# TensorE's order in an attention loop: both halves of the value products between two pairs of score tiles

## The chip, the cores and the metric

The kernel runs on 1 core of one Trainium2 chip. The metric is device time in microseconds of one execution, lower is better; the figure given is the median of several executions.

## What is computed

A pre-norm attention block followed by a pre-norm FFN with values rounded to fp8, on x of shape (4, 1024, 128), 16 heads of size 8:

```
proj = layernorm(x) @ w_in;  k, v, q = split(proj)
scores = q k^T / sqrt(8) + tisa_bias(head, j - i)      # the bias depends on j - i alone
attn   = softmax(scores) v
x = x + a * sigmoid(g),  (a, g) = split(attn @ w_gate + b_gate)
x = x + ffn(layernorm(x))                              # 128x128, both operands rounded to fp8
```

The change lies in the loop that makes scores, their softmax numerators and the products with v.

## The kernel before

A **group** is 128 keys of one head, for all 4 batches and all 1024 queries of each. A head has 8 groups (`GPH`), 16 heads make 128 groups. The loop `Fori(0, NH2)` on every engine takes two heads (16 groups) a turn, 8 turns. Numbers within a group are the batches b = 0 to 3.

Work of a group, and who does it:

- TensorE, `scores(i, g, b)`, L909 to L940: for one batch two matmuls (L928), one for each half of the queries, into two PSUM banks. For b = 0, 1, 2 ("by vector", `DPG` = 3) the tile goes alternately to banks 0-1 and 2-3 (`unit(k)`, k counts such tiles). Before tile k TensorE waits (L920) until VectorE has read tile k-2, for the same banks. For b = 3 the tile goes to banks 4-5, after a wait (L924) for ScalarE's exponential of b = 3 of the group before; four more matmuls (L937) then add the bias as identity times the table `t64`. I call these "the identity bias".
- VectorE, `add_bias`, L987: for b = 0, 1, 2 reads the score tile from PSUM, adds the bias table and writes to a buffer in SBUF (`pbuf` or `split`, 4 groups deep, `SETS`).
- ScalarE: exponential in place for b = 0, 1, 2 (L1030), and from PSUM for b = 3 (L1038), strictly in the order 0, 1, 2, 3.
- TensorE, `products(i, g, c)`, L942 to L959: for one half c of the queries, 4 matmuls of fp32 data (each one recorded as two), one for each batch, v (with a column of ones for the denominators) against the exponentials, accumulated over the head's 8 groups in bank 6+c. c = 0 waits (L946) for the exponentials of the whole group; for the first group of a head each half also waits (L951) until the sums of the last head have been copied out of the bank.

TensorE runs scores two groups ahead of products (`LAG` = 2): at step g it issues the scores of group g+2 and the products of group g. Within a step its order is written out by hand at L967: score tile 0, products half 0, score tile 1, products half 1, score tiles 2 and 3 with the identity bias. Each engine's queue runs in order; nothing behind a waiting instruction of TensorE starts before it.

Once per head VectorE copies bank 6 (L779, after half 0 of the head's last products, `half_done`) and ScalarE copies bank 7 (L780, after half 1). SyncE and GpSimd load the next head's tables and normalise the last head's sums; none of that is touched.

Of the kernel before, what the change touches and what calls it, by code (L numbers as in the profile page):

```python
# [62 lines left out]
def attention_block(nc, io, out):  # L63
    with ExitStack() as ctx:
# [238 lines left out]
        with nc.Block() as block:  # L303
# [91 lines left out]
            def _(eng):  # L395
# [41 lines left out]
                def bias_copies(_):  # L437
                    eng.wait_ge(gsum_ready, 1)
                    eng.activation(gvh[:, :], ps[:, 0, :], ACT.Copy).then_inc(gh_ready, 1)
                    eng.activation(gv[:, :], ps[:, 0, :], ACT.Copy).then_inc(gh_ready, 1)  # L440
# [5 lines left out]
                def high_keys(_):  # L446
                    eng.wait_ge(kh_ready, B)
                    load_keys(eng, 2, (0, 8), 1)
# [344 lines left out]
        def slot(g, b):  # L793

            n = 4 * (g % SETS) + b
            return pbuf[:, n, :] if n < 8 else splitf[:, (n - 8) * S:(n - 7) * S]

        def unit(k):

            return 2 * (k % 2)  # L800
# [16 lines left out]
        with nc.Block() as block:  # L817
# [89 lines left out]
            @block.tensor  # L907
            def _(eng):
                def scores(i, g, b):  # L909

                    p, t = (g // GPH) % 2, g % GPH
                    by_vector = b < DPG
                    if b == 0 and t == 0:
                        eng.wait_ge(head_in[p], (i + (g // (2 * GPH))) * (16 * LOADS) + 16 * LOADS)
                    if by_vector:
                        k = DPG * g + b
                        u = unit(k)

                        if k >= 2:
                            eng.wait_ge(z_ready, i * (2 * DPH) + (k - 1))  # L920
                    else:
                        u = 4
                        if g:
                            eng.wait_ge(p_ready, i * (8 * GPH) + 4 * g)  # L924
                    keys = slice(b * S + t * P, b * S + (t + 1) * P)
                    for c in range(2):
                        rows = slice(ROW * c, ROW * c + 33)
                        last = eng.matmul(ps[:, u + c, :], kb[p][rows, keys],  # L928
                                          qb[p][rows, b * HALF:(b + 1) * HALF],
                                          start=True, stop=True)  # L930
                    if by_vector:
                        last.then_inc(sd_ready, 1)
                        return
                    for c in range(2):
                        for m in range(2):
                            c0 = t * P + 64 * m + c * HALF
                            last = eng.matmul(ps[64 * m:64 * m + 64, u + c, :], ident2[:, :],  # L937
                                              t64[p][:, c0:c0 + HALF], start=False, stop=True,
                                              skip_group_check=True)
                    last.then_inc(sp_ready, 1)  # L940

                def products(i, g, c):  # L942

                    p, t = (g // GPH) % 2, g % GPH
                    if c == 0:
                        eng.wait_ge(p_ready, i * (8 * GPH) + 4 * (g + 1))  # L946
                        if t == 0:
                            eng.wait_ge(vst_in, i * 2 + (p + 1))
                    if t == 0:

                        eng.wait_ge(o_ready[c], i * 2 + (p + 1))  # L951
                    for b in range(B):
                        last = eng.matmul(ps[32 * b:32 * b + 32, 6 + c, :], vst[p][:, b * TB + t, :],  # L953
                                          slot(g, b)[:, c * HALF:(c + 1) * HALF],
                                          start=(t == 0), stop=(t == TB - 1))
                    if c == 1:
                        last.then_inc(groups_done, 1)
                    elif t == TB - 1:
                        last.then_inc(half_done, 1)  # L959

                for g in range(LAG):
                    for b in range(B):
                        scores(0, g, b)
                with eng.Fori(0, NH2) as i:
                    for g in range(2 * GPH):

                        for steps, c in (((0,), 0), ((1,), 1), ((2, 3), None)):  # L967
                            if g < 2 * GPH - LAG:
                                for b in steps:
                                    scores(i, g + LAG, b)  # L970
                            else:

                                with eng.If(i < NH2 - 1):
                                    for b in steps:
                                        scores(i, g + LAG, b)
                            if c is not None:
                                products(i, g, c)

            @block.vector
# [578 lines left out]
```

## Time and profile before

| what | us |
|---|---|
| median of 3 executions | 625.23 |
| lowest, highest | 624.38, 629.33 |
| the profiled execution | 625.92 |
| its span in the trace | 624.1 |

The rows of the profile are given further down. They name engines as PE (TensorE's matmuls), PEld (its weight loads), DVE (VectorE), ACT (ScalarE), POOL (GpSimd) and SP (SyncE). A matmul row merges the matmuls of one kind that follow each other: x8 of L953 is one half of the products of one group, x2 of L928 is one score tile. The loop's score groups start at 68.5 us of the span, and its last products end at 562 us.

### The profile page before, as it was taken

The page shows a single profiled execution, that of the slowest core. Times are in us where ns is not written, and L with a number is a line of the kernel's source. Part 1 is how long each engine was busy: PE and PEld are TensorE (multiplying, and loading weights), DVE is VectorE, ACT ScalarE, POOL GpSimd, SP SyncE. Part 2 cuts the span into 40 slices and gives each one's busy share as a digit, 9 for nine tenths or more (in the row PEclk, how much of TensorE's full clock was granted, in tenths as well). Part 3 has the DMA queues.
Part 4 walks back from the last instruction along what each step waited for, and adds up shares of the span by engine and source line. Part 5 has one row for each costly group of instructions (what it writes and reads, how often), then busy time and mean ns, then how long its engine had stood idle before and what let it go on. Part 6 is the DMA issues. An engine that isn't in the chain of part 4 may idle for free.

```text
span 624.1 us, 12700 instructions
## 1 busy us (share of the span) xinstructions
PE 576.9 (92%) x4003; PEld 157.9 (25%) x4003; DVE 552.1 (88%) x691; ACT 553.4 (89%) x615; POOL 88.3 (14%) x90
## 2 busy tenths in 40 slices
PE   4887499999999999999999999999999999999945
PEld 1534012222222222222222222222222222224532
DVE  6763599999999999999999999999999999974885
ACT  5663499999999999999999999999999999983475
POOL 4170400010101010101010101001010101011640
PEclk8797599999999999999999999999999999999958
DMA  7117620514141424232332323231414141410004
GB/s 178 67 22 206 223 65 2 149 20 148 32 133 42 123 59 109 79 90 87 81 102 63 104 61 110 55 117 49 121 45 123 43 133 39 124 23 9 1 0 135
DMA packets 29484, 52.63 MB, mean 84 GB/s; under 512 B 9438, under 2 KB 20699, under 8 KB 28507
## 3 DMA queue, kind: packets, MB, share of 16 engines
q1 hardware_dynamic: 27496, 51.70, 29.2%
q10 hardware_dynamic: 1970, 0.73, 0.6%
q8 instruction: 8, 0.13, 0.1%
q14 instruction: 10, 0.07, 0.0%
HBM read 42.35 MB, written 9.16 MB: 83 GB/s over the span
## 4 chain that ended last, share of the span: by engine, by line
ACT 43%; issue 36%; PE 9%; DVE 4%; SPq 3%; DMA 2%; ACTq 1%; DVEq 0%
ACT split L1030 17%; ACT pbuf L1030 17%; ACT pbuf L1038 3%; PE ps L1232 3%; ACT split L1038 2%; PE ps L585 1%; SPq L301 1%; DMA amp<-in_L_attn_amplitudes 1%; DMA kb<-split 1%; SPq L262 1%; PE ps L953 1%; PE ps L1227 1%; ACT o_sbs L780 1%; PE ps L928 1%; PE ps L575 1%
## 5 line engine op out<-in xcount | busy, mean ns | idle before, releaser
L987 DVE TENSOR_TENSOR split<-ps,t 128x1024 f32<-128x1024 f32 x192 | 231.4, 1222 | 13.0 <-PE ps L928 7.6
L987 DVE TENSOR_TENSOR pbuf<-ps,t 128x1024 f32<-128x1024 f32 x192 | 230.2, 1217 | 11.8 <-PE ps L928 6.9
L1030 ACT ACTIVATE pbuf<-pbuf 128x1024 f32<-128x1024 f32 x192 | 206.7, 1255 | 8.6 <-DVE pbuf L987 8.3
L1030 ACT ACTIVATE split<-split 128x1024 f32<-128x1024 f32 x192 | 202.2, 1263 | 1.2 <-DVE split L987 1.2
L928 PE MATMUL ps<-qb,kb 33*128 33x512 f16 x1024 | 184.1, 390 | 13.3 <-SPq L845 6.4
L953 PE MATMUL ps<-pbuf,vst 128*32 128x512 f32 x1024 | 137.2, 608 | 0.0
L953 PE MATMUL ps<-split,vst 128*32 128x512 f32 x1024 | 136.0, 604 | 1.0 <-ACT split L1038 1.0
L928 PEld LDWEIGHTS ps<-qb,kb 33*128 33x128 f16 x1024 | 48.6, 93 | 300.7 <-DVE pbuf L987 114.1
L937 PE MATMUL ps<-t64s,ident 128*64 128x512 f16 x512 | 80.5, 395 | 0.0
L1038 ACT ACTIVATE split<-ps 128x1024 f32<-128x1024 f32 x64 | 78.3, 1223 | 0.0
L1038 ACT ACTIVATE pbuf<-ps 128x1024 f32<-128x1024 f32 x64 | 77.9, 1218 | 0.0
L905 POOL TENSOR_TENSOR o_sbs<-o_sbs,rd 128x1024 f32<-128x1024 f32 x8 | 19.1, 2390 | 179.6 <-DMA rd<-r_scratch 179.6
L899 POOL TENSOR_TENSOR o_sbs<-o_sbs,rd 128x1024 f32<-128x1024 f32 x7 | 16.7, 2388 | 157.9 <-DMA rd<-r_scratch 157.9
L953 PEld LDWEIGHTS ps<-split,vst 128*32 128x32 f32 x1024 | 20.3, 108 | 31.5 <-issue 29.7
L953 PEld LDWEIGHTS ps<-pbuf,vst 128*32 128x32 f32 x1024 | 20.2, 108 | 29.2 <-issue 29.2
L937 PEld LDWEIGHTS ps<-t64s,ident 128*64 128x64 f16 x512 | 18.1, 108 | 31.2 <-issue 31.2
L277 POOL COPY vst<-v_all 128x256 f32 (+1 forms) x16 | 6.4, 398 | 120.0 <-PE ps L953 98.3
L1314 ACT ACTIVATE pbuf<-ps 128x256 f32<-128x256 f32 x16 | 6.0, 381 | 14.8 <-PE ps L1232 14.8
L1232 PE MATMUL ps<-wgate,v_all 128*128 128x256 f32 x64 | 18.1, 405 | 0.0
L1164 POOL TENSOR_TENSOR x_sb<-x_sb,pbuf 128x256 f32<-128x256 f32 x16 | 11.5, 724 | 29.1 <-DVE pbuf L1431 29.1
L1431 DVE TENSOR_TENSOR pbuf<-ps,pbuf 128x256 f32<-128x256 f32 x16 | 6.6, 415 | 8.9 <-ACT pbuf L1314 8.9
L780 ACT ACTIVATE o_sbs<-ps 128x512 f32<-128x512 f32 x16 | 12.7, 792 | 2.0 <-PE ps L953 2.0
(151 smaller groups left out, 325.4 us busy)
## 6 DMA issues: line engine op xcount, KB each, us to landing
t<-g_scratch SPq DMA_DIRECT2D x16, 960.0 KB
kb<-k_scratch SPq DMA_DIRECT2D x120, 64.0 KB
t64s<-gh_scratch SPq DMA_DIRECT2D x16, 248.0 KB
t64s<-gl_scratch SPq DMA_DIRECT2D x16, 248.0 KB
qb<-q_scratch SPq DMA_DIRECT2D x60, 64.0 KB
x_sb<-in_L_attn_x SPq DMA_DIRECT2D x4, 512.0 KB, 7.6
q_scratch<-split SPq DMA_DIRECT2D x8, 256.0 KB, 3.9
k_scratch<-split SPq DMA_DIRECT2D x8, 256.0 KB, 3.8
```

Of the source, the lines that this page charges most:

```text
L780: return eng.activation(dst, src, ACT.Copy)
L899: eng.tensor_tensor(o_sb[1], o_sb[1], rd[:, :], ALU.mult).then_inc(o_norm, 1)
L905: eng.tensor_tensor(o_sb[0], o_sb[0], rd[:, :], ALU.mult).then_inc(o_norm, 1)
L928: last = eng.matmul(ps[:, u + c, :], kb[p][rows, keys], qb[p][rows, b * HALF:(b + 1) * HALF], start=True, stop=True)
L937: last = eng.matmul(ps[64 * m:64 * m + 64, u + c, :], ident2[:, :], t64[p][:, c0:c0 + HALF], start=False, stop=True, skip_group_check=True)
L953: last = eng.matmul(ps[32 * b:32 * b + 32, 6 + c, :], vst[p][:, b * TB + t, :], slot(g, b)[:, c * HALF:(c + 1) * HALF], start=(t == 0), st ...
L987: eng.tensor_tensor(slot(g, b), banks(unit(k), 2), t128[p][:, t * P:t * P + S], ALU.add).then_inc(z_ready, 1)
L1030: eng.activation(buf, buf, ACT.Exp).then_inc(p_ready, 1)
L1038: eng.activation(buf, banks(4, 2), ACT.Exp).then_inc(p_ready, 1)
L1164: eng.tensor_tensor(xs, xs, gate[:, j % NG, :], ALU.add).then_inc(x1_ready, 1)
L1232: last = eng.matmul(ps[:, j % 4, m * 2 * D:(m + 1) * 2 * D], num[n // TB][:, (n % TB) * P:(n % TB + 1) * P], wgate[:, :], start=False, sto ...
L1431: eng.tensor_tensor(gate[:, j % NG, :].rearrange("p (m d) -> p m d", d=D), ps[:, j % 4, :].rearrange("p (m c) -> p m c", c=2 * D)[:, :, 0: ...
```

## The change

Within a step TensorE issues score tiles 0 and 1 together, then both halves of the products, then score tiles 2 and 3 and the identity bias. The waits stay with the functions that issue them, the number of instructions of each kind is the same, and no other engine's program changes.

```
-                        for steps, c in (((0,), 0), ((1,), 1), ((2, 3), None)):
+                        for steps, halves in (((0, 1), (0, 1)), ((2, 3), ())):
                             if g < 2 * GPH - LAG:
                                 for b in steps:
                                     scores(i, g + LAG, b)
@@
                                 with eng.If(i < NH2 - 1):
                                     for b in steps:
                                         scores(i, g + LAG, b)
-                            if c is not None:
+                            for c in halves:
                                 products(i, g, c)
```

## Rows read from the trace of the kernel before

**Rows 1.** The page's first part: busy time of each engine, its share of the span

```profile
PE 576.9 (92%) x4003; PEld 157.9 (25%) x4003; DVE 552.1 (88%) x691; ACT 553.4 (89%) x615; POOL 88.3 (14%) x90
```

**Rows 2.** The page's groups: busy, mean ns of one, idle before and its releaser

```profile
L987 DVE TENSOR_TENSOR pbuf<-ps,t 128x1024 f32<-128x1024 f32 x192 | 230.2, 1217 | 11.8 <-PE ps L928 6.9
```

**Rows 3.** Windows: length, busy of PE, PEld, DVE, ACT, POOL, clock, DMA share, GB/s

```profile
68.50:76.50 8.00, 5.97 (x24) 1.06 (x24) 6.71 (x6) 5.80 (x6) 4.32 (x6) 0.50 0.64 237
150.00:300.00 150.00, 148.31 (x1104) 32.94 (x1102) 144.76 (x129) 150.00 (x164) 13.94 (x10) 1.00 0.30 84
```

**Rows 4.** Timeline of PE over one step: start us, length us, then the instructions

```profile
304.77 0.63 PE L928 MATMUL ps<-qb,kb 33*128 33x512 f16 x4
305.33 0.62 PE L937 MATMUL ps<-t64s,ident 128*64 128x512 f16 x4
305.89 0.39 PE L928 MATMUL ps<-qb,kb 33*128 33x512 f16 x2
306.21 1.06 PE L953 MATMUL ps<-pbuf,vst 128*32 128x512 f32 x8
307.20 0.39 PE L928 MATMUL ps<-qb,kb 33*128 33x512 f16 x2
307.52 1.06 PE L953 MATMUL ps<-pbuf,vst 128*32 128x512 f32 x8
308.52 0.39 PE L928 MATMUL ps<-qb,kb 33*128 33x512 f16 x2
```

**Rows 5.** Timeline, narrow windows in the same step: single instructions of PE, ACT, DVE

```profile
305.01 0.39 PE L928 MATMUL ps<-qb,kb 33*128 33x512 f16 x2
303.68 1.28 ACT L1038 ACTIVATE pbuf<-ps 128x1024 f32<-128x1024 f32 x1
305.21 1.23 DVE L987 TENSOR_TENSOR pbuf<-ps,t 128x1024 f32<-128x1024 f32 x1
306.41 1.22 DVE L987 TENSOR_TENSOR split<-ps,t 128x1024 f32<-128x1024 f32 x1
```

**Rows 6.** Timeline, early in the loop: PE's tile 0, and ACT's L1038

```profile
81.42 0.39 PE L928 MATMUL ps<-qb,kb 33*128 33x512 f16 x2
103.78 0.39 PE L928 MATMUL ps<-qb,kb 33*128 33x512 f16 x2
82.98 1.01 ACT L1038 ACTIVATE split<-ps 128x1024 f32<-128x1024 f32 x1
105.45 1.03 ACT L1038 ACTIVATE pbuf<-ps 128x1024 f32<-128x1024 f32 x1
```

**Rows 7.** Timeline at the loop's end: both halves of the last products, and DVE's copy

```profile
560.17 1.92 PE L953 MATMUL ps<-split,vst 128*32 128x512 f32 x16 [0.95 <-ACT split L1038]
561.30 0.69 DVE L779 COPY o_sbs<-ps 128x512 f32<-128x512 f32 x1 [3.47 <-PE ps L953]
```

**Rows 8.** Timeline: a score tile of PE that waited for DVE

```profile
106.43 1.22 DVE L987 TENSOR_TENSOR pbuf<-ps,t 128x1024 f32<-128x1024 f32 x1
107.70 0.39 PE L928 MATMUL ps<-qb,kb 33*128 33x512 f16 x2
```

**Rows 9.** Timeline around the two copies at a head's end, DVE and ACT

```profile
440.75 0.68 DVE L779 COPY o_sbs<-ps 128x512 f32<-128x512 f32 x1
441.35 2.34 DVE L987 TENSOR_TENSOR pbuf<-ps,t 128x1024 f32<-128x1024 f32 x2
441.53 1.32 ACT L1030 ACTIVATE pbuf<-pbuf 128x1024 f32<-128x1024 f32 x1
442.96 1.33 ACT L1030 ACTIVATE pbuf<-pbuf 128x1024 f32<-128x1024 f32 x1
```

**Rows 10.** Timeline at the low clock: a score tile, half 0, the next score tile

```profile
76.53 0.61 PE L928 MATMUL ps<-qb,kb 33*128 33x512 f16 x2
77.06 1.93 PE L953 MATMUL ps<-pbuf,vst 128*32 128x512 f32 x8
78.93 0.47 PE L928 MATMUL ps<-qb,kb 33*128 33x512 f16 x2
```

More of the change, by code:

```diff
@@ L965, in _ @@
                     for g in range(2 * GPH):
-                        for steps, c in (((0,), 0), ((1,), 1), ((2, 3), None)):
+                        for steps, halves in (((0, 1), (0, 1)), ((2, 3), ())):
                             if g < 2 * GPH - LAG:
@@ L975, in _ @@
                                         scores(i, g + LAG, b)
-                            if c is not None:
+                            for c in halves:
                                 products(i, g, c)
```

## The prediction

> **What bounds the kernel now.** I read the page first, then windows by stage, then the timeline of single steps. The page shows three engines that are nearly even: PE 92%, DVE 88%, ACT 89% of the span [rows 1], and DVE's adds have little idle before them, 11.8 us for 192 of them [rows 2]. An average can't tell which of them is the bound, so I looked at the windows: in 150 us of the loop PE is busy for 148.31, ACT for all 150.00, DVE for 144.76, at clock 1.00 [rows 3]. The loop is the place to look; the change touches nothing outside it.
>
> The timeline of one step gives its shape. Call score tiles S0 to S3, the identity bias I, the halves P0 and P1. From S2 at 304.77 to the next S2 at 308.52 are 3.75 us, and PE goes through it without a hole: S2 to S3 0.24 (305.01), S3 to I 0.32, I to S0 0.56, S0 to P0 0.32, P0 to S1 0.99, S1 to P1 0.32, P1 to S2 1.00 [rows 4, 5]. Is PE the bound? Early in the loop it ran by itself: S0 at 81.42 and at 103.78 are 6 groups apart, 3.73 us a group. Over the same groups ACT's L1038 ended at 83.99 and at 106.48: 22.49 us for 6, 3.75 a group [rows 6]. So ACT is the slower one; it fell behind until S3, which needs the banks that ACT reads in L1038, had to wait for it: ACT ends at 303.68 + 1.28 = 304.96, S3 starts at 305.01 [rows 5]. From then on all go at ACT's 3.75, with PE only 0.02 faster on its own. DVE has the most room: back to back its adds start 1.13 apart (two in 2.34, the second taking 1.21 [rows 9]), and 1.20 where it goes from S2 to S0 (305.21 to 306.41 [rows 5]), 3.46 a group.
>
> Per head the copies add to this. ACT starts its next exponential at 442.96, 1.43 after the one at 441.53, where a quarter of a group is 0.94: 0.49 later [rows 9]. A head takes about 8 x 3.75 + 0.49 = 30.5 us.
>
> **What the change does to PE's own time.** Nothing is added or removed, no DMA or other queue is passed. Four neighbour pairs change. Before: S0-P0, P0-S1, S1-P1, P1-S2. After: S0-S1, S1-P0, P0-P1, P1-S2. S0 to S1 now costs what S2 to S3 does, 0.24. P0 with P1 directly behind exists at the loop's end: 16 records in 1.92 against 1.06 for one half [rows 7, 4], so the second half adds 0.86; and since a half of 1.06 is followed by the next score tile 1.00 after its start, both take 1.86 from P0's start to S2. PE's own step becomes 0.24 + 0.32 + 1.86 + 0.24 + 0.32 + 0.56 = 3.54, against 3.75: 0.21 saved.
>
> The Trainium skill ("TensorEngine Tiling (Array Packing)", Key Properties) says that a change of tiling mode drains TensorE, and scores and products here differ in mode; the rows fit, with 0.99 from half to score tile where half to half is 0.86. By that rule with PE as the bound the loop's 125 steps would give back 26 us. The rule is not wrong, but the time saved is not on the path, for two reasons.
>
> First, ACT needs 3.75 a group whatever PE does. So a quicker PE alone gives nothing.
>
> Second, and this decides, the new order puts a wait at a bad place. S1 is tile k+2 to S2 of the group before (the order on DVE's banks is S0, S1, S2, S0', S1'), so S1' needs the banks of S2, which DVE must have read (L920). Count from S2's start:
>
> - S2 to DVE's start on it: 304.77 to 305.21, 0.44 as read; 0.43 is what single records and the step's sums agree on [rows 4, 5]
> - DVE's add: 1.23 [rows 5]
> - DVE's end to the score tile that waits for it: 106.43 + 1.22 = 107.65 to 107.70, 0.05 [rows 8]
>
> So S1' cannot start before S2 + 1.71. Before the change it started at S2 + 2.43 (307.20), since P0 stood ahead of it: 0.72 of slack, the wait was free. After, PE is ready for it at 0.24 + 0.32 + 0.56 + 0.24 = 1.36 and stands still for about 0.35 to 0.4. Behind it in the queue stand P0 and P1, whose data is long there, and behind them S2', which is what DVE needs next. So a closed chain forms:
>
> S2 -0.43-> DVE -1.23-> -0.05-> S1' -0.32-> P0, P1 -1.86-> S2': 3.89 us a group.
>
> DVE has S0' and S1' to do meanwhile: S0' starts at 0.43 + 1.20 = 1.63, S1' at 2.76, and DVE could take S2' at 3.89, but gets it at 3.89 + 0.43 = 4.32. It idles 0.4 a group, PE about 0.35 to 0.4, ACT 0.14. Before, the longer way round (S2' 3.75 after S2) never closed, as two small waits lay apart.
>
> Could another wait bite as well? S2' needs DVE to be done with S0': 1.63 + 1.22 = 2.85, it starts at 3.89. S3' needs ACT's L1038. ACT can take S2's tile at 1.7, then L1038 0.94 later, done by 2.64 + 1.28 = 3.92 at the longest length seen; S3' is due at 3.89 + 0.24 = 4.13. P0 needs exponentials of two groups earlier, more than 3 us old. None bites.
>
> **Sum.** The loop issues scores for groups 2 to 127, so 125 intervals from S2 to S2. 118 go from 3.75 to 3.89: +16.5. The first seven went at 3.73: 7 x 0.16 = +1.1. The head's end happens 15 times in the loop: DVE's copy of bank 6 waits for P0, which ends later now. P0 starts at S2 + 1.71 + 0.32 = 2.03; at the loop's end the copy started 1.13 after P0 did [rows 7], so at 3.16. After the copy DVE's add follows 0.60 later (440.75 to 441.35), the one for S2' 1.13 behind it [rows 9]: 4.89 instead of 4.32. That is +0.57 a head, and ACT's copy (0.49) fits under it. The old cost of 0.49 goes, so 15 x 0.08 = +1.2. The first step of the loop, at the low clock, has two switches fewer: about -0.2. Together **+18.6 us**. The profiled execution took 625.92, so 644.5; it lies 0.7 above the median of 625.23, which goes to **644 us**.
>
> Bounds. If going from half 0 to half 1 within the loop costs as a change of weights between two passes does, 0.45 twice instead of 0.43 (1.06 less the last record's 0.61), 0.05 more a group: +6, 650. The two handoffs (0.43 and 0.05) are each seen with an error of 0.02: 125 x 0.04 = 5 either way. If the copy waits for nothing new, 1.2 less. Both low ends together give 638, both high ends 655; as the rows of the loop's end show the two halves directly, I cut the top to 652.
>
> **Rivals.**
>
> - *The wait costs nothing, the time stays (625).* It needs the closed chain under 3.75, that is 0.14 shorter than its rows. For: PE gains 0.21 a step. Against: each term was read where it stands alone, and the chain holds no part of what PE gains except P0-P1. Then ACT at 3.75 decides and no time is won. Chance 7%.
> - *PE was the bound, the switches' time is won.* Place: the changes between score and product; price 0.21 x 125 = 26, so 599 (the page on tiling would have it so); it decides only if ACT can go under 3.75, and DVE's chain too. In no group did ACT do so [rows 6]. Chance 2%.
> - *The clock falls.* PE stands still 0.35 to 0.4 us each 3.89. At clock 0.50, while PE was busy 5.97 of 8.00 us [rows 3], a half took 1.87 to the next score tile (77.06 to 78.93), tile to half 0.53, and a tile's record 0.61 for 0.39 [rows 10, 4], so S2 to DVE 0.43 + 0.22: a step would take about 0.53 + 2 x 1.87 + 0.65 + 1.23 + 0.05 = 6.2 us. One group in ten at that clock adds 12.5 x 2.3 = 29 us: 673. Against: PE will still be busy some 93% of each step, in even pieces. Chance 4%. The Trainium skill ("TensorE: Matmul & The Clock Gate", A second HAM failure mode: psum-queue depth-cycling) tells of a kernel whose small idles between groups of matmuls for want of PSUM banks made the clock swing; that is this rival's case, and the trace of before has no such swing in the loop.
> - *The chain holds but with another length, outside 638 to 652.* For instance, DVE's late copy delays two steps of a head, not one (another 15 x 0.4 = 6), or PE's loads restart slower after a real stall. Chance 12%.
>
> My forecast, the closed chain at 3.84 to 3.94: 75%. What this kernel's measurement can tell from no change is about 1%. Slower by over 1%: 75 + 4 + 12 = 91, less 1 for a chain much shorter than thought, 90%. Same 8%, faster 2%.
>
> **What the profile of after would show.** Steps 3.89 apart from S2 to S2. PE idle of about 0.35 to 0.4 ahead of S1 in every step, released by DVE L987, with S1 0.05 behind DVE's end on S2's tile. PE's busy in 150:300 down from 148 to about 140. Idle of DVE before its adds to `pbuf` up from 11.8 us [rows 2] to 25 to 32, released by PE L928. ACT no longer busy all the time, its L1038 records back from 1.28 [rows 5] to the 1.01 to 1.03 of the first groups [rows 6], since nothing queues in it. S0 to S1 0.24, P0 and P1 as one row of 16 with 1.92. Wrong would be: S1 ahead of DVE's end by more than the wait allows, steps of 3.75 with ACT still full, or a granted clock under 1.00 inside the loop.

## The result, and the profile after

The changed kernel took 646.69 us (median of 4, 645.96 to 649.2) against 625.87 for the kernel before in the same session (median of 4): a ratio of 1.033, with an interval of 1.030 to 1.036. So it is 3.3% slower. The forecast was 644 us, 638 to 652. One execution of the kernel before, in the session of e1, e3, e4 and e5, took 2132.34 us and is left out of the ratios.

The profiled execution has a span of 644.5 us, 20.4 more than before. The page's first part, and the groups that answer to [rows 1] and [rows 2]:

```profile
PE 563.8 (87%) x4003; PEld 160.3 (25%) x4003; DVE 544.9 (85%) x691; ACT 569.1 (88%) x615; POOL 88.3 (14%) x90
...
L987 DVE TENSOR_TENSOR pbuf<-ps,t 128x1024 f32<-128x1024 f32 x192 | 226.8, 1216 | 22.2 <-PE ps L928 21.5
L928 PE MATMUL ps<-qb,kb 33*128 33x512 f16 x1024 | 178.9, 388 | 46.9 <-DVE pbuf L987 24.1
```

TensorE lost 13 us of busy time and yet the span grew. VectorE waits 22.2 us for score tiles (L928) before its adds to `pbuf`, where it waited 11.8 us before [rows 2], and TensorE's score tiles wait for VectorE: each waits for the other, which is what a closed chain looks like in the groups. The window answers to [rows 3]; its columns are the same:

```profile
150.00:300.00 150.00, 138.68 (x1062) 32.55 (x1054) 136.81 (x123) 148.71 (x157) 13.91 (x10) 1.00 0.26 74
```

PE fell from 148.31 to 138.68, DVE from 144.76 to 136.81, ACT from 150.00 to 148.71, at clock 1.00 as before. No engine is full any more; ScalarE's 148.71 still looks full, but the length of its records is not its pace (last section). One step on the timelines of PE and DVE, against [rows 4, 5]:

```profile
441.57 0.61 PE L928 MATMUL ps<-qb,kb 33*128 33x512 f16 x4
442.10 0.62 PE L937 MATMUL ps<-t64s,ident 128*64 128x512 f16 x4
442.66 0.39 PE L928 MATMUL ps<-qb,kb 33*128 33x512 f16 x2
443.28 0.39 PE L928 MATMUL ps<-qb,kb 33*128 33x512 f16 x2 [0.23 <-DVE pbuf L987]
443.60 1.92 PE L953 MATMUL ps<-pbuf,vst 128*32 128x512 f32 x16
445.46 0.39 PE L928 MATMUL ps<-qb,kb 33*128 33x512 f16 x2
442.00 1.23 DVE L987 TENSOR_TENSOR pbuf<-ps,t 128x1024 f32<-128x1024 f32 x1 [0.36 <-PE ps L928]
443.18 2.36 DVE L987 TENSOR_TENSOR split<-ps,t 128x1024 f32<-128x1024 f32 x2
445.89 1.23 DVE L987 TENSOR_TENSOR split<-ps,t 128x1024 f32<-128x1024 f32 x1 [0.35 <-PE ps L928]
```

S2 starts at 441.57. VectorE takes it at 442.00 (0.43 later) and is done at 443.23 (1.23). S1 starts at 443.28 (0.05), the halves at 443.60 (0.32), the next S2 at 445.46 (1.86). The sum is the step: 3.89. The chain that ended last, cut to 430 to 450 us, by line:

```profile
by line: PE ps L953 46.3%; DVE split L987 24.7%; PE ps L928 20.0%; DVE pbuf L987 12.4%; issue 1.8%
```

It runs through the products, the adds and the score tiles, the terms of the sum; ScalarE has no part in it.

### The profile page after: what moved, and what is told of

The parts are those of the page before. It is cut to its first block, busy times and chain, and to the rows that moved or that the text cites. A ratio compares the mean times of both kernels' runs of the same rounds, so it can differ in the third digit from the quotient of the medians.

```text
span 644.5 us, 12684 instructions
## 1 busy us (share of the span) xinstructions
PE 563.8 (87%) x4003; PEld 160.3 (25%) x4003; DVE 544.9 (85%) x691; ACT 569.1 (88%) x615; POOL 88.3 (14%) x90
## 4 chain that ended last, share of the span: by engine, by line
PE 58%; DVE 29%; issue 5%; SPq 3%; DMA 2%; ACT 2%; DVEq 0%; ACTq 0%
PE ps L953 35%; PE ps L928 14%; DVE pbuf L987 13%; DVE split L987 12%; PE ps L1232 2%; PE ps L1276 1%; PE ps L585 1%; SPq L301 1%; DMA amp<-in_L_attn_amplitudes 1%; DMA kb<-split 1%; SPq L262 1%; PE ps L1227 1%; PE ps L575 1%; DVE amax L1462 1%; DMA v_all<-last_rows 1%
## 5 line engine op out<-in xcount | busy, mean ns | idle before, releaser
L987 DVE TENSOR_TENSOR pbuf<-ps,t 128x1024 f32<-128x1024 f32 x192 | 226.8, 1216 | 22.2 <-PE ps L928 21.5
L928 PE MATMUL ps<-qb,kb 33*128 33x512 f16 x1024 | 178.9, 388 | 46.9 <-DVE pbuf L987 24.1
L1030 ACT ACTIVATE pbuf<-pbuf 128x1024 f32<-128x1024 f32 x192 | 197.2, 1052 | 11.1 <-DVE pbuf L987 8.2
L1030 ACT ACTIVATE split<-split 128x1024 f32<-128x1024 f32 x192 | 195.4, 1052 | 3.8 <-DVE split L987 2.1
L953 PE MATMUL ps<-pbuf,vst 128*32 128x512 f32 x1024 | 124.8, 606 | 0.0
L953 PE MATMUL ps<-split,vst 128*32 128x512 f32 x1024 | 123.1, 598 | 0.7 <-ACT split L1038 0.7
L928 PEld LDWEIGHTS ps<-qb,kb 33*128 33x128 f16 x1024 | 39.2, 93 | 246.7 <-issue 139.9
L1038 ACT ACTIVATE pbuf<-ps 128x1024 f32<-128x1024 f32 x64 | 64.5, 1007 | 0.0
L1038 ACT ACTIVATE split<-ps 128x1024 f32<-128x1024 f32 x64 | 64.5, 1007 | 0.0
L953 PEld LDWEIGHTS ps<-pbuf,vst 128*32 128x32 f32 x1024 | 26.9, 110 | 53.8 <-issue 53.8
L953 PEld LDWEIGHTS ps<-split,vst 128*32 128x32 f32 x1024 | 26.7, 109 | 54.4 <-issue 52.3
L779 DVE COPY o_sbs<-ps 128x512 f32<-128x512 f32 x16 | 11.1, 692 | 8.4 <-PE ps L953 8.4
```

What stands on the lines that cost most here:

```text
L779: return eng.tensor_copy(dst, src)
L928: last = eng.matmul(ps[:, u + c, :], kb[p][rows, keys], qb[p][rows, b * HALF:(b + 1) * HALF], start=True, stop=True)
L987: eng.tensor_tensor(slot(g, b), banks(unit(k), 2), t128[p][:, t * P:t * P + S], ALU.add).then_inc(z_ready, 1)
L1030: eng.activation(buf, buf, ACT.Exp).then_inc(p_ready, 1)
L1038: eng.activation(buf, banks(4, 2), ACT.Exp).then_inc(p_ready, 1)
```

## The experiments

All times below are medians, and the kernel before is 625.22 to 627.53 in the runs beside them. "Head's end" is the step in which the last sums of a head are copied out.

### Is it the wait behind VectorE's add? (e3)

```
# from the changed kernel; VectorE, then ScalarE
+                    w = HALF if b == 2 else S
-                    eng.tensor_tensor(slot(g, b), banks(unit(k), 2), t128[p][:, t * P:t * P + S],
+                    eng.tensor_tensor(slot(g, b)[:, 0:w], banks(unit(k), 2)[:, 0:w], t128[p][:, t * P:t * P + w],
...
-                                eng.activation(buf, buf, ACT.Exp).then_inc(p_ready, 1)
+                                eng.activation(buf, buf, ACT.Exp, scale=0.0 if b == 2 else 1.0).then_inc(p_ready, 1)
```

> The changed kernel, but VectorE adds the bias for the first 512 of 1024 columns of tile 2 only, and ScalarE's exponential of tile 2 (still 1024 columns) has scale 0, so its values are all 1: part of the computation is left out. Theory (closed chain): VectorE's add of tile 2 falls from 1.23 to about 0.69 and the chain from 3.89 to 3.35, below ScalarE's 3.75, which then sets the step as before the change, with 0.49 more at each head's end: 625, 622 to 629. TensorE waits for ScalarE ahead of S3, not for VectorE ahead of S1. Rival (the halves together are slow in themselves, or ScalarE is slowed by the new order): 647, as ScalarE and TensorE have the same work.

Measured: 626.75 us, a ratio to the kernel before of 1.000 (0.998 to 1.002). All of the loss is gone, though TensorE and ScalarE have the same instructions to do. The timeline of PE; the fifth line is a narrow window that shows S3 alone:

```profile
431.41 0.61 PE L928 MATMUL ps<-qb,kb 33*128 33x512 f16 x4
431.94 1.92 PE L953 MATMUL ps<-pbuf,vst 128*32 128x512 f32 x16
433.80 0.87 PE L928 MATMUL ps<-qb,kb 33*128 33x512 f16 x4
434.60 0.62 PE L937 MATMUL ps<-t64s,ident 128*64 128x512 f16 x4
434.28 0.39 PE L928 MATMUL ps<-qb,kb 33*128 33x512 f16 x2
435.16 0.39 PE L928 MATMUL ps<-qb,kb 33*128 33x512 f16 x2
```

S0 and S1 follow each other without a hole; the only wait is S3's for its banks (S3 starts 0.48 behind S2, 433.80 to 434.28, where 0.23 would do without a wait), and the step is 3.75 (431.41 to 435.16). With the chain shortened, ScalarE sets the step again, as in the kernel before. This shows that the chain through VectorE's add costs the time, not the halves standing together in themselves. It also shows that the new order gains nothing while ScalarE needs 3.75.

### Does the new order save TensorE anything? (e4, e5)

```
# e4 from the changed kernel, e5 from the kernel before: the cuts of e3, and
+                                w = HALF if b == 1 else S
+                                eng.activation(buf[:, 0:w], buf[:, 0:w], ACT.Exp,
+                                               scale=0.0 if b == 2 else 1.0).then_inc(p_ready, 1)
```

> As the last kernel, and ScalarE's exponential of tile 1 is done for 512 of 1024 columns only: part of the computation is left out. With the chain at 3.35 and ScalarE at about 3.3 a step, TensorE's own time sets the step. Theory (the new order does save TensorE 0.21 to 0.23 a step): 0.23 + 0.32 + 1.86 + 0.23 + 0.31 + 0.24 + 0.31 = 3.50 a step, 125 x 0.25 = 31 us under 625, and some of the 15 x 0.49 of ScalarE's copy covered: 588, 584 to 598. Rival (changing between scores and products costs nothing that the order can save): as e5, near 616.

> The kernel before the change, with the same two cuts (VectorE's add of tile 2 and ScalarE's exponential of tile 1 for 512 columns only, the exponential of tile 2 with scale 0): part of the computation is left out. TensorE's own time with the old order sets the step: 3.73, as in groups 3 to 9 of the kernel before. 118 x 0.02 = 3 less, and ScalarE's copy of 0.49 at 15 head ends is covered: 7 less: 616, 612 to 620. e4 should lie 22 to 30 us below it, 125 steps of 0.21 to 0.23. Rival: both the same.

Measured: e4 593.35, e5 615.37 us; ratios to the kernel before 0.946 (0.943 to 0.949) and 0.983 (0.978 to 0.987). With VectorE's and ScalarE's limits lifted, the new order is the quicker by 22 us. PE's timeline of e4, then of e5:

```profile
401.63 0.61 PE L928 MATMUL ps<-qb,kb 33*128 33x512 f16 x4
402.17 1.92 PE L953 MATMUL ps<-split,vst 128*32 128x512 f32 x16
404.02 0.61 PE L928 MATMUL ps<-qb,kb 33*128 33x512 f16 x4
...
405.12 0.39 PE L928 MATMUL ps<-qb,kb 33*128 33x512 f16 x2
```

```profile
415.93 0.39 PE L928 MATMUL ps<-qb,kb 33*128 33x512 f16 x2
416.25 1.07 PE L953 MATMUL ps<-split,vst 128*32 128x512 f32 x8
417.25 0.39 PE L928 MATMUL ps<-qb,kb 33*128 33x512 f16 x2
417.57 1.06 PE L953 MATMUL ps<-split,vst 128*32 128x512 f32 x8
...
419.65 0.39 PE L928 MATMUL ps<-qb,kb 33*128 33x512 f16 x2
```

A step is 3.49 (401.63 to 405.12) against 3.72 (415.93 to 419.65). TensorE's saving is real, 0.23 to 0.24 a step: 125 x 0.24 = 30 us. Of this 8 us go back at the heads' ends: in e4 the step from 415.57 takes 3.64 and the one from 419.20 takes 3.86 against 3.48 of the others, so 0.54 a head and 15 x 0.54 = 8; in e5 the same steps take 3.73 like all. This cost at the heads' ends is why e4 came out at 593 and not at 588.

### Is it where the two halves stand, or S0 with S1? (e1)

```
-                        for steps, halves in (((0, 1), (0, 1)), ((2, 3), ())):
+                        for steps, halves in (((0,), (0, 1)), ((1, 2, 3), ())):
```

> Order in a step: S0, P0, P1, S1, S2, S3, I; no other change. The pair that the change put together, S0 with S1, is apart again; both halves still stand together. Theory (closed chain through VectorE's two pairs of banks): the tile ahead of the halves is now S0 and the tile behind them S1, and S0' needs the banks of S1. S1 to VectorE 0.43, add 1.23, 0.05 to S0', 0.32 to P0, 1.86 to S1': 3.89 us a step again, with TensorE's wait ahead of S0 in place of S1. Here S1, S2 and S3 follow each other, so ScalarE's exponential of tile 3 ends late: S1 + 0.43 + 1.23 + 0.03 (exponential of tile 1), 1.13 later tile 2, 0.95 later tile 3, 1.01 long, 0.06 to the next S3: that S3 starts at 4.84 in place of 4.34, and a step takes (4.84 + 0.86 + 2.18) / 2 = 3.94. The copy at a head's end is hidden more than in the changed kernel (about 0.3 for 0.67). Sum: 125 x 0.05 - 15 x 0.37 = +1 on the 646.7 of the changed kernel: 648, 642 to 653. Rival (the loss comes from S0 and S1 standing together ahead of the products): back to about 625.

Measured: 648.45 us, a ratio of 1.034 (1.031 to 1.037), the same loss as the changed kernel's, and 648 was worked out. PE's timeline over two steps:

```profile
444.06 0.39 PE L928 MATMUL ps<-qb,kb 33*128 33x512 f16 x2
444.38 1.92 PE L953 MATMUL ps<-pbuf,vst 128*32 128x512 f32 x16
446.23 0.61 PE L928 MATMUL ps<-qb,kb 33*128 33x512 f16 x4
447.19 0.39 PE L928 MATMUL ps<-qb,kb 33*128 33x512 f16 x2 [0.35 <-ACT pbuf L1038]
...
448.06 0.39 PE L928 MATMUL ps<-qb,kb 33*128 33x512 f16 x2
...
450.24 0.61 PE L928 MATMUL ps<-qb,kb 33*128 33x512 f16 x4
451.08 0.39 PE L928 MATMUL ps<-qb,kb 33*128 33x512 f16 x2 [0.23 <-ACT split L1038]
...
451.95 0.39 PE L928 MATMUL ps<-qb,kb 33*128 33x512 f16 x2
```

S0 starts at 444.06, 448.06 and 451.95: steps of 4.00 and 3.89 in turn, mean 3.95, where 3.94 was worked out. S3 waits for ScalarE in both, for longer in the 4.00 (0.35 in the records against 0.23). So the mean step here is set by the longer way round that was worked out before the run: from S1 over VectorE's add and three exponentials to S3 of the next step, and from there over both halves to S1 of the step after. The chain through VectorE alone lies just under it: in the shorter steps S0 comes 1.71 behind S1 (450.24 to 451.95), which is its 0.43 + 1.23 + 0.05. That S0 and S1 are apart again brings nothing back. What the two orders share is that both halves stand between two neighbouring VectorE tiles.

### Does work count more inside the chain? (e2)

```
-                        for steps, halves in (((0, 1), (0, 1)), ((2, 3), ())):
+                        for steps, halves in (((0, 1), (0, 1)), ((3, 2), ())):
```

> The changed kernel with tiles 2 and 3 exchanged: S0, S1, P0, P1, S3, I, S2. TensorE has the same instructions and nearly the same own time, about 3.5 a step. Theory (closed chain): S3 and I now lie between the halves and S2, inside the chain: S3 to I 0.31, second pair of I 0.24, to S2 0.32, so 0.86 more a step: 4.75. At the head's end VectorE's copy is hidden by VectorE's longer idle, 15 x 0.67 less. 646.7 + 108 - 10 = 745, 735 to 755. Rival (the time is TensorE's work plus a fixed cost of the halves standing together): no change, 647.

Measured: two runs only, 774.31 us with a mean granted clock of 0.93 and 797.40 us with 0.90, beside 625.22 us for the kernel before with 0.95 to 0.96. Both are more than the 735 to 755 expected; the profile is of the longer one. PE's timeline, first of a step at the full clock, then of one that ran partly at the low clock; then two windows (columns as in [rows 3]):

```profile
600.06 0.60 PE L928 MATMUL ps<-qb,kb 33*128 33x512 f16 x4
601.77 0.39 PE L928 MATMUL ps<-qb,kb 33*128 33x512 f16 x2 [1.11 <-DVE split L987]
602.09 1.92 PE L953 MATMUL ps<-pbuf,vst 128*32 128x512 f32 x16
603.95 0.39 PE L928 MATMUL ps<-qb,kb 33*128 33x512 f16 x2
604.27 0.62 PE L937 MATMUL ps<-t64s,ident 128*64 128x512 f16 x4
604.82 0.60 PE L928 MATMUL ps<-qb,kb 33*128 33x512 f16 x4
...
429.64 0.60 PE L928 MATMUL ps<-qb,kb 33*128 33x512 f16 x4
431.35 0.39 PE L928 MATMUL ps<-qb,kb 33*128 33x512 f16 x2 [1.11 <-DVE pbuf L987]
431.67 3.39 PE L953 MATMUL ps<-pbuf,vst 128*32 128x512 f32 x16
436.05 0.61 PE L928 MATMUL ps<-qb,kb 33*128 33x512 f16 x4
...
432.00:435.30 3.30, 3.30 (x18) 0.54 (x10) 1.56 (x2) 3.19 (x4) 1.12 (x1) 0.50 0.16 22
150.00:600.00 450.00, 354.88 (x2432) 79.86 (x2432) 312.99 (x283) 341.56 (x359) 29.82 (x22) 0.92 0.22 63
```

At clock 1.00 the step is 4.76 (600.06 to 604.82); 4.75 was worked out: the same instructions, 0.87 a step longer, since the identity bias now lies between the halves and S2. TensorE stands idle 1.11 us a step. And here what was a rival of the prediction happened: the clock fell. In the step from 429.64 to 436.05 the clock was 0.50 from 432.0 to 435.3, the lower of its two levels (1.2 and 2.4 GHz); the halves took 3.39 for 1.92, and the step 6.41. Over 150 to 600 us the mean clock was 0.92 with PE busy 79% of the time. After the loop's first step, 29 steps are of that kind, 6.3 to 6.5 us each; together they cost 48 us of the profiled run's 797, and without them it would be about 750, inside the range expected. From 575 to 664 us the steps were of the same 4.76 us and the clock stayed at 1.00; what decides when it falls, these runs do not show.

### The head's end (e6)

```
# VectorE, for both heads of a turn; from the changed kernel
-                            if b == 0 and g == LAG - 1:
+                            if b == 1 and g == LAG - 1:
...
-                            if b == 0 and g == GPH + LAG - 1:
+                            if b == 1 and g == GPH + LAG - 1:
```

> The changed kernel, with VectorE's copy of bank 6 at a head's end put after its add of tile 1 in place of tile 0; the computation is the same. By the trace of the changed kernel each head's end costs 0.67 over a plain step, since VectorE stands idle until half 0 is done before it can copy. Theory: after tile 1 half 0 is long done, the copy (0.61) falls into VectorE's idle time of 0.42 ahead of tile 2, and 0.19 is left: 15 x 0.48 = 7 less: 639.5, 637 to 643. Rival (the 0.67 comes from ScalarE's copy of bank 7): 646 to 648.

Measured: 639.98 us, a ratio of 1.022 (1.019 to 1.024), so 6.7 us less than the changed kernel (7 us by the two ratios, 1.033 and 1.022, each taken against the kernel before in its own session). First VectorE around the copy in the changed kernel, then in e6:

```profile
456.49 0.69 DVE L779 COPY o_sbs<-ps 128x512 f32<-128x512 f32 x1 [0.42 <-PE ps L953]
457.10 2.35 DVE L987 TENSOR_TENSOR pbuf<-ps,t 128x1024 f32<-128x1024 f32 x2
```

```profile
452.50 0.68 DVE L779 COPY o_sbs<-ps 128x512 f32<-128x512 f32 x1
453.09 1.21 DVE L987 TENSOR_TENSOR pbuf<-ps,t 128x1024 f32<-128x1024 f32 x1
```

In the changed kernel VectorE stood 0.42 in front of the copy, waiting for half 0 (L953), with the adds behind it. In e6 the copy starts without a wait. The heads' ends cost 0.67 each before and 0.15 to 0.25 now, by the distances between S0s over two steps. ScalarE's copy was not touched, so it was not the cause.

## Why the prediction was right

**The bound of the kernel before.** Argued from ScalarE's pace in the first groups; shown by e3 (ScalarE alone holds the step at 3.75 when the chain is short) and by e5 (with less work for ScalarE and VectorE the old order runs at 3.72 to 3.73, TensorE's own time, which was forecast as 3.73).

**TensorE's own saving.** Forecast 0.21 a step; e4 against e5 shows 0.23 to 0.24. The small miss is that S0 to S1 and S2 to S3 take 0.23 and S3 to the identity bias 0.31 where nothing waits; the row of before, with 0.24 and 0.32, had S3 waiting. The Trainium skill ("TensorEngine Tiling (Array Packing)", Key Properties) says that a change of tiling mode drains TensorE. The runs agree so far as fewer changes between scores and products are worth 0.23 to 0.24 a step; whether a drain is what costs it, they do not show. In the changed kernel the time was lost all the same, which was the point of the two reasons given.

**The closed chain.** Term by term: S2 to VectorE 0.43 (forecast 0.43), add 1.23 (1.23), to S1 0.05 (0.05), to the halves 0.32 (0.32), both halves 1.86 (1.86); the step 3.89 (3.89). This carried 17.6 of the 18.6 us forecast. e3 and e2 test it from two sides: a term shortened, and the chain lengthened by 0.86. e1 moves it by one tile and rules out that S0 with S1 costs the time, but its mean step is set by the longer way round through ScalarE, so it is no test of the 3.89.

**The head's end.** This term was sized too small. Forecast was 0.57 a head, 0.67 is measured. TensorE's timeline has the parts:

```profile
455.27 1.92 PE L953 MATMUL ps<-split,vst 128*32 128x512 f32 x16
457.13 0.61 PE L928 MATMUL ps<-qb,kb 33*128 33x512 f16 x4
459.50 0.39 PE L928 MATMUL ps<-qb,kb 33*128 33x512 f16 x2 [0.74 <-DVE pbuf L987]
```

The copy starts at 456.49, 1.22 after the first half's start (455.27), where the loop's end had 1.13 [rows 7]. So the row taken for it did not hold within the loop, by 0.09; the rest is rounding. 15 x 0.10 = 1.5 us, which is nearly all of what the profiled execution took beyond the forecast (20.4 against 18.6). Why the copy comes 0.09 later in the loop than at its end, no run here shows. The step of the sum was right in kind, as e6 shows by taking most of it away.

**The first step.** Forecast -0.2. The loop's first score tile came 0.88 earlier (67.67 against 68.55) and the first step was longer, since both halves ran at the low clock in it:

```profile
67.67 0.61 PE L928 MATMUL ps<-qb,kb 33*128 33x512 f16 x2 [6.67 <-SPq L845]
...
76.60 3.64 PE L953 MATMUL ps<-pbuf,vst 128*32 128x512 f32 x16
80.18 0.45 PE L928 MATMUL ps<-qb,kb 33*128 33x512 f16 x2
```

S2 started at 80.18, and at 80.33 before: -0.15. The sum is right by luck: the earlier start and the longer step, neither of them forecast, nearly cancel.

**The signs that were named.** PE's wait was to be 0.35 to 0.4 ahead of S1: S1 comes 0.62 after S0 (442.66 to 443.28) and 0.23 would do, so 0.39. Its record shows 0.23, as S0's record of 0.39 covers the rest. The wait of VectorE before its adds to `pbuf` was to grow to 25 to 32 us; it is 22.2. The forecast counted 0.43 a step between starts (4.32 less 3.89), but the records of two adds overlap by 0.09, so only 0.35 shows. The sign "S0 to S1 0.24" left out the wait that the forecast itself put there; 0.62 is measured. The clock stayed at 1.00 in the loop after its first step.

**The rivals.** That the wait would cost nothing is excluded by the timeline. That TensorE was the bound is excluded by e3, where the new order waits for ScalarE at 3.75 a step. The falling clock did not come in the changed kernel but did in e2, with 1.11 us idle in the records of a step against 0.23. It is a real risk of this kind of change. The Trainium skill ("TensorE: Matmul & The Clock Gate", A second HAM failure mode: psum-queue depth-cycling) tells of a kernel that cycles through PSUM banks and in which short idles of TensorE between groups of matmuls made the clock swing between its two levels. The trace of e2 agrees, with stretches at 0.50 and at 1.00 in turn; that of the changed kernel has no such swing from 150 to 570 us.

## What to carry to other kernels

When two buffers stand between a producer and a consumer, walk round the circle: consumer's start, its work, the handoff back, and everything that the producer's in-order queue has between the tile that waits and the next tile that the consumer needs. If that sum exceeds the step of the busiest engine, it is the step, whatever the engines' busy times say. Walk the circles that take two steps as well, and halve them: in e1 such a one was the longer. Grouping like work to save switches lengthens just this stretch: it pays where the producer itself is the bound (e4), and costs where it makes a long block without a tile for the consumer.

## What the runs showed of the hardware

- What follows a half of the products decides what it costs: from its start 1.00 to a score tile [rows 4], 0.86 to the other half, in the loop as at its end. A half after a score tile starts 0.32 behind it, another score tile 0.23. Together these are the 0.23 a step that e4 shows.
- An idle time of TensorE of 0.23 us in every 3.89 left the granted clock at 1.00 from 150 to 570 us; with one of 1.11 in every 4.76 it fell to 0.50 again and again, with a mean of 0.92, and the steps in which it fell took up to 6.46. With the same steps it also stayed at 1.00 for 89 us on end.
- ScalarE's exponential from PSUM (L1038) is recorded with 1.28 us in the kernel before [rows 5], where ScalarE is behind, and with 1.01 in the changed kernel, where it keeps up, for the same work. So the length of a record is not the time that ScalarE needs for the work: it was longer where ScalarE was behind. Its busy time of 150.00 in 150 us was therefore no proof that it was the bound, just as 148.71 in the changed kernel, where it isn't on the chain, is none; the pace over six groups [rows 6] and e3 tell more.
